# Query and key parts laid out head by head in DRAM, with two buffers in two attention stages and the query stores issued by ScalarE

## The reference, cut to what matters

```
q = (layernorm(x) @ Wq + bq), k = (ctx @ Wk + bk), v = (ctx @ Wv + bv)   # 8 x 512 x 256, 16 heads of 16
scores = einsum('bhqd,bhkd->bhqk', q, k) * scale                        # per head 512 x 512
out = softmax(scores) @ v                                               # then @ Wo + bo, added to x
```

## Time and profile before

| | us |
|---|---|
| median of 3 runs | 4700.8 (4699.31 to 4715.89) |
| the profiled execution | 4706.52 |
| its span | 4704.8 |
| a0: projections, then first work of the loop | 10.5 to 175.0 |
| a2: the same | 2925.2 to 3080.2 |
| a3: the same | 3831.2 to 3986.8 |

### The profile page before, as it was taken

One profiled execution on the slowest core, in us unless ns is written; L12 is line 12 of the kernel. 1 busy time (PEld: TensorE's weight loads), 2 busy tenths in 40 slices (PEclk: granted clock), 3 DMA queues, 4 the chain that ended last, 5 costly groups with the idle time before them and its releaser, 6 DMA issues. The chain is left out here.

```text
span 4704.8 us, 82799 instructions
## 1 busy us (share of the span) xinstructions
PE 3914.7 (83%) x30525; PEld 2826.9 (60%) x30525; DVE 3099.6 (66%) x7110; ACT 2060.3 (44%) x3636; POOL 796.3 (17%) x510
## 2 busy tenths in 40 slices
PE   6599999699367999785499996669988974999899
PEld 5244444588365777674388885535555663455577
DVE  7466664546656666545466664668867884988687
ACT  2155555134113333342154443247776851677511
POOL 4333330501341000000023323210000021000000
PEclk8699999599668999897599998869998997899999
DMA  6333331201320000010244545412210024121100
GB/s 205 102 98 101 101 96 41 88 21 44 106 77 32 18 18 18 28 43 31 72 126 123 130 125 144 166 60 66 67 37 14 1 71 148 55 66 65 34 19 19
DMA packets 202874, 337.94 MB, mean 72 GB/s; under 512 B 26036, under 2 KB 119781, under 8 KB 202566
## 3 DMA queue, kind: packets, MB, share of 16 engines
q1 hardware_dynamic: 186680, 306.61, 20.4%
q0 software_dynamic: 15888, 27.23, 2.8%
HBM read 242.42 MB, written 107.01 MB: 74 GB/s over the span
## 5 line engine op out<-in xcount | busy, mean ns | idle before, releaser
L1904 ACT ACTIVATE a_pT<-a_psS 128x512 f32<-128x512 f32 x1536 | 835.9, 598 | 405.0 <-PE a_psS L1790 399.6
L1976 DVE TENSOR_REDUCE a_mx<-a_psA 128x1 f32<-128x512 f32 x1024 | 656.6, 685 | 88.1 <-PE a_psA L1768 87.8
L1768 PE MATMUL a_psA<-a_ks,a_qs 48*128 48x512 f32 (+1 forms) x1536 | 404.4, 522 | 160.9 <-PEq L46 59.0
L1805 PE MATMUL a_psZ<-a_pT,a_V 128*17 128x128 f32 x12288 | 488.4, 278 | 0.0
L1972 DVE CUSTOM_DVE_ANT_0 a_scored<-a_psA,a_hide_q 128x512 bf16<-128x512 f32 x512 | 332.6, 688 | 193.4 <-PE a_psA L1768 192.3
L1805 PEld LDWEIGHTS a_psZ<-a_pT,a_V 128*17 128x17 f32 x12288 | 272.6, 97 | 270.8 <-issue 161.7
L1768 PEld LDWEIGHTS a_psA<-a_ks,a_qs 48*128 48x128 f32 (+1 forms) x1536 | 151.2, 192 | 408.7 <-issue 176.0
L1790 PE MATMUL a_psS<-a_qs,a_ks 50*128 50x512 f32 (+1 forms) x1536 | 319.1, 409 | 3.2 <-ACT a_pT L1904 0.8
L3244 DVE SCALAR_TENSOR_TENSOR ex_h<-ex_psU,ex_ub,ex_sg 128x512 f32<-128x512 f32 x129 | 96.9, 751 | 188.6 <-PE ex_psU L159 181.6
L1988 POOL TENSOR_TENSOR X<-X,a_osb 128x512 f32<-128x512 f32 x48 | 61.2, 1280 | 941.1 <-ACT a_osb L1891 923.1
L3190 ACT CAST ex_w_h<-X 128x1024 fp32r<-128x1024 f32 x102 | 106.1, 1041 | 149.3 <-DMA X<-in_L_ffn_gw 145.3
(11 more groups left out here) (606 smaller groups left out, 10257.4 us busy)
## 6 DMA issues: line engine op xcount, KB each, us to landing
a_k_parts<-a_p_kp SPq DMA_DIRECT2D x96, 256.0 KB
a_q_parts<-a_p_qp SPq DMA_DIRECT2D x96, 256.0 KB
a_qs<-a_q_parts SPq DMA_DIRECT2D x192, 128.0 KB
a_ks<-a_k_parts SPq DMA_DIRECT2D x192, 128.0 KB
X<-in_L_ffn_gw SPq DMA_DIRECT2D x36, 512.0 KB, 4.5
X<-in_L_ffn_up_w SPq DMA_DIRECT2D x36, 512.0 KB, 3.3
X<-in_L_ffn_down_w SPq DMA_DIRECT2D x36, 512.0 KB, 3.8
top_rows<-blank_rows SPq DMA_DIRECT2D x32, 514.0 KB, 11.3
```

The costliest lines, as they stand in the source:

```text
L1768: nc.tensor.matmul(psA[:, unit(a, par) % 3], qs[r, g % ring, p % 2, q * P:(q + 1) * P], ks[r, g % ring, p % 2], start=True, stop=True).the ...
L1805: last = nc.tensor.matmul(psZ[q * VP:q * VP + VW, g % 2, j * P:(j + 1) * P], V[:, b, kt, g % NG * GH + j, :], pT[:, p % 2, par, kt, q * P: ...
L1904: nc.scalar.activation(pT[:, p % 2, par, kt, :], psS[:, unit(t, par) % 3], ACT.Exp).then_inc(exp_done, 1)
L1976: nc.vector.tensor_reduce(mx[:, p // 2 % 2, par, p % 2, q:q + 1], psA[:, unit(a, par) % 3], AX_X, ALU.max).then_inc(a_used, 1)
```

## The change

In DRAM, `q_parts` and `k_parts` have the head ahead of the feature. A store then writes 128 consecutive rows. A load of a group has three DMAs for each stack and half in place of two: each takes one part of two heads, so none reads its source twice; 12 DMAs of 64 KB in place of 4 of 128 KB and 4 of 64 KB. In a2 and a3 `kp` and `qp` have two buffers, with a semaphore for each; a0 keeps one. The stores of the queries move from SyncE's program to ScalarE's, behind the copy of the next batch's tokens (`scalar_high`) and a wait for the low part of Q.

```diff
@@ resident_projections
-        kp, qp = sb("kp", [P, 2, KD, S], F32R), sb("qp", [P, 2, KD, S], F32R)
+        kp, qp = sb("kp", [P, buffers, 2, KD, S], F32R), sb("qp", [P, buffers, 2, KD, S], F32R)
...
+        def store(eng, parts, dram, stored):
+            for n in range(2):
+                for m in range(KD):
+                    heads = dram[n, m * P // DH:(m + 1) * P // DH].rearrange("h d t -> (h d) t")
+                    eng.dma_start(heads, parts[:, n, m].bitcast(F32)).then_inc(stored, 16)
...
-                            heads = dram[n, :, m * P // DH:(m + 1) * P // DH].rearrange("d h t -> h d t")
-                            sp.dma_start(heads, parts[:, n, m].bitcast(F32)).then_inc(stored, 16)
...
                     sp.wait_ge(k_low, b + 1)
-                    store(kp, k_dram[:, b], k_stored)
-                    sp.wait_ge(q_low, b + 1)
-                    store(qp, q_dram[:, b], q_stored)
+                    store(sp, kp[:, b % buffers], k_dram[:, b], k_stored[b % buffers])
                     if b == 4:
-                        sp.wait_ge(k_stored, 64 * b)
-                        sp.wait_ge(q_stored, 64 * b)
+                        for stored in k_stored + q_stored:
+                            sp.wait_ge(stored, 64 * b // buffers)
                     prepare.loads(sp, b)
...
                 def high_part(in_psum, ps, parts, bias, stored, done, b):
                     act.wait_ge(in_psum, b + 1)
-                    if b >= 1:
-                        act.wait_ge(stored, 64 * b)
+                    if b >= buffers:
+                        act.wait_ge(stored[b % buffers], 64 * (b // buffers))
...
                     high_part(q_in_psum, psQ, qp, bqs, q_stored, q_high, b)
                     if b + 1 < B:
                         f.scalar_high(act, b + 1, 0)
+                    act.wait_ge(q_low, b + 1)
+                    store(act, qp[:, b % buffers], q_dram[:, b], q_stored[b % buffers])
@@ attention_by_pairs
-        q_dram = nc.dram_tensor(nm + "q_parts", [2, B, DH, H, S], F32).ap()
-        k_dram = nc.dram_tensor(nm + "k_parts", [2, B, DH, H, S], F32).ap()
+        q_dram = nc.dram_tensor(nm + "q_parts", [2, B, H, DH, S], F32).ap()
+        k_dram = nc.dram_tensor(nm + "k_parts", [2, B, H, DH, S], F32).ap()
...
-                    return dram[part:part + 1, b, :, first:first + 2].rearrange("r d h t -> r d (h t)")
-                for stack, start, src in ((qs, 0, heads(q_dram, 0).to_broadcast([2, DH, 2 * S])), (qs, 2 * DH, heads(q_dram, 1)),
-                                          (ks, 0, heads(k_dram, 1)), (ks, DH, heads(k_dram, 0).to_broadcast([2, DH, 2 * S]))):
-                    rows = slice(64 * par + start, 64 * par + start + src.shape[0] * DH)
-                    sp.dma_start(stack[rows, slot].bitcast(F32).rearrange("p j t -> p (j t)"), src).then_inc(group_loaded[slot], 16)
+                    return dram[part, b, first:first + 2].rearrange("h d t -> d h t")
+                for stack, third, src in ((qs, 0, heads(q_dram, 0)), (qs, 1, heads(q_dram, 0)), (qs, 2, heads(q_dram, 1)),
+                                          (ks, 0, heads(k_dram, 1)), (ks, 1, heads(k_dram, 0)), (ks, 2, heads(k_dram, 0))):
+                    rows = slice(64 * par + third * DH, 64 * par + (third + 1) * DH)
+                    sp.dma_start(stack[rows, slot].bitcast(F32), src).then_inc(group_loaded[slot], 16)
...
+        (the call: buffers = 1 if hidden is not None else 2)
```

More of the change, by code:

```diff
@@ L1350, with resident_projections @@
 LEAD = 2 * STEPS
-def resident_projections(nc, A, G, nm, w, q_scale, q_dram, k_dram, V, wo, bo, prepare):
+def resident_projections(nc, A, G, nm, w, q_scale, q_dram, k_dram, V, wo, bo, buffers, prepare):
     with ExitStack() as ctx:
@@ L1369, in resident_projections @@
         cT_h, cT_l = sb("cT_h", [P, 2, KD, S], F32R), sb("cT_l", [P, 2, KD, S], F32R)
-        kp, qp = sb("kp", [P, 2, KD, S], F32R), sb("qp", [P, 2, KD, S], F32R)
+        kp, qp = sb("kp", [P, buffers, 2, KD, S], F32R), sb("qp", [P, buffers, 2, KD, S], F32R)
         w_loaded = {n: sem(n + "_loaded") for n in names}
         w_high, w_low, small_loaded, scaled = sem("w_high"), sem("w_low"), sem("small_loaded"), sem("scaled")
-        cT_loaded, k_stored, q_stored = [sem("cT_loaded0"), sem("cT_loaded1")], sem("k_stored"), sem("q_stored")
+        cT_loaded, k_stored, q_stored = [sem("cT_loaded0"), sem("cT_loaded1")], [sem(f"k_stored{n}") for n in range(buffers)], [sem(f"q_stored{n}") for n in range(buffers)]
         cT_high, cT_low, k_in_psum, v_in_psum, q_in_psum, v_taken, k_high, k_low, q_high, q_low = (
@@ L1394, in _ @@
                 prepare.sync(sp)
-                def store(parts, dram, stored):
-                    for n in range(2):
-                        for m in range(KD):
-                            heads = dram[n, :, m * P // DH:(m + 1) * P // DH].rearrange("d h t -> h d t")
-                            sp.dma_start(heads, parts[:, n, m].bitcast(F32)).then_inc(stored, 16)
                 for b in range(B):
@@ L1406, in _ @@
                     sp.wait_ge(k_low, b + 1)
-                    store(kp, k_dram[:, b], k_stored)
-                    sp.wait_ge(q_low, b + 1)
-                    store(qp, q_dram[:, b], q_stored)
+                    store(sp, kp[:, b % buffers], k_dram[:, b], k_stored[b % buffers])
                     if b == 4:
-                        sp.wait_ge(k_stored, 64 * b)
-                        sp.wait_ge(q_stored, 64 * b)
+                        for stored in k_stored + q_stored:
+                            sp.wait_ge(stored, 64 * b // buffers)
                     prepare.loads(sp, b)
-                sp.wait_ge(k_stored, 64 * B)
-                sp.wait_ge(q_stored, 64 * B)
+                for stored in k_stored + q_stored:
+                    sp.wait_ge(stored, 64 * B // buffers)
                 sp.wait_ge(small_loaded, 16 * len(smalls))
@@ L1466, in high_part @@
                     act.wait_ge(in_psum, b + 1)
-                    if b >= 1:
-                        act.wait_ge(stored, 64 * b)
+                    if b >= buffers:
+                        act.wait_ge(stored[b % buffers], 64 * (b // buffers))
                     for m in range(KD):
-                        nc.scalar.activation(parts[:, 0, m, :], ps[:, m, :], ACT.Identity, bias=bias[:, m:m + 1]).then_inc(done, 1)
+                        nc.scalar.activation(parts[:, b % buffers, 0, m, :], ps[:, m, :], ACT.Identity, bias=bias[:, m:m + 1]).then_inc(done, 1)
                 f.scalar_roots(act, 0)
@@ L1505, in low_part @@
                         dve.wait_ge(high_done, 2 * b + m + 1)
-                        last = nc.vector.scalar_tensor_tensor(parts[:, 1, m, :], ps[:, m, :], bias[:, m:m + 1],
-                                                              parts[:, 0, m, :].bitcast(F32), ALU.add, ALU.subtract)
+                        last = nc.vector.scalar_tensor_tensor(parts[:, b % buffers, 1, m, :], ps[:, m, :], bias[:, m:m + 1],
+                                                              parts[:, b % buffers, 0, m, :].bitcast(F32), ALU.add, ALU.subtract)
                     last.then_inc(done, 1)
@@ L1550, in attention_by_pairs @@
     ROWS = max_row + 2
-    LOADS = 2 * (4 + (added is not None))
+    LOADS = 2 * (6 + (added is not None))
     ring = 4 if hidden is not None else 5
     with ExitStack() as ctx:
-        q_dram = nc.dram_tensor(nm + "q_parts", [2, B, DH, H, S], F32).ap()
-        k_dram = nc.dram_tensor(nm + "k_parts", [2, B, DH, H, S], F32).ap()
+        q_dram = nc.dram_tensor(nm + "q_parts", [2, B, H, DH, S], F32).ap()
+        k_dram = nc.dram_tensor(nm + "k_parts", [2, B, H, DH, S], F32).ap()
         sb = lambda n, s, d=F32: ctx.enter_context(nc.sbuf_tensor(nm + n, s, d))
@@ L1680, in prepare_loads @@
                 load_group(sp, b - 4)
-        resident_projections(nc, A, G, nm + "p_", w, q_scale, q_dram, k_dram, V, wo, bo,
+        resident_projections(nc, A, G, nm + "p_", w, q_scale, q_dram, k_dram, V, wo, bo, 1 if hidden is not None else 2,
                              Prepare(prepare_sync, prepare_loads, prepare_pool, prepare_vector))
```

## The result

The changed kernel takes 4570.7 us in the median of four runs (4567.7 to 4572.8), beside 4702.5 for the kernel before in the same session: a ratio of 0.971, 95% interval 0.969 to 0.973. The forecast was 4570. The profiled execution took 4569.46 us with a span of 4567.5, against a span of 4704.8 before.

The account below looks back on a forecast made before the run. Projection halves wait for DMA, stores on 8 engines and doubled loads on two. Terms 46 + 45 + 33 + 7 + 6.6 = 137.6, less 7 for queueing, 130.6; 4700.8 - 130.6 = 4570 us, range 4540 to 4625.

Parts of the forecast that it names:

- a share of 0.57: Early a2 batches: DMA share 0.57 at 199 GB/s means 9.1 engines' worth, stores on 8 engines, a period of 13.1 us.
- The rate, 21.8 GB/s an engine: Early a2 batches: 199 GB/s over 9.1 engines' worth of work, used for the transfer times.
- the second period: a2 once loads come in: kp copies 20.9 us apart; doubled loads on two engines, 560 KB in 21 us at 27 GB/s.
- Halves of a2 and a3: Projection halves: batches of 11.1 us and a shorter stretch from last root to loop save 46 and 45 us.
- What would have shown it: Signs: a2 kp copies 11 us apart without DMA waits, share about 0.65 at over 230 GB/s, under 30 us root to loop.
- Predicted 33: a0's half: earlier mask makes the last qp some 20 us earlier, tail of 10.1 replaces 22.9: together 33 us saved.
- One buffer was called enough: a0's half: a key store would land some 5 us after issue, 2 us before the next copy is due.
- ScalarE's issues: Projections: four query issues at 565 to 630 ns take 2.3 to 2.5 us, fit into 3.34 us before the root, cost nothing.
- The bound named for the other side: Projections: at the crowded 5.98 us for four, ScalarE's query issues cost 2.6 us in each of 21 periods, 55 us.
- slower rival: Loops of a2 and a3: SyncE becomes the bound, 12 issues at over 0.94 us; 4725 us or more, chance 0.03.
- Loops: Attention loops: spread loads save 6.6 us in a0 and 7 in a3, whose four groups take 50.2 us; a2 nothing.
- the 7 us of queueing: Taken off the summed gain: 0.3 us in each of 21 periods.

Follow-up runs that it names:

- experiment 5: A kernel that only moves data, output x: outermost numbers 128, 16, 12, 8, 4, 2 gave DMA shares 1.03, 1.00, 0.76, 0.52, 0.26, 0.13.
- experiment 3: The changed kernel with an unused row behind each head in DRAM, so stores write 8 x 16 rows again: 4645.8 us, ratio 0.987.
- experiment 4: The changed kernel with eight of its twelve 64 KB loads a group reading their source twice again: 4636.6 us, ratio 0.985.
- Experiment 8: The changed kernel with single kp and qp buffers in a2 and a3 too: 4566.8 us, ratio 0.970.
- experiment 1: The kernel before with the new layout alone (head-by-head tensors, merged stores, twelve loads), single buffers, query stores on SyncE: 4568.6 us, ratio 0.971.
- experiment 7: The changed kernel with the query stores back on SyncE, both buffers kept: 4581.1 us, ratio 0.973.
- experiment 6: The changed kernel again, unaltered, measured beside other variants: 4563.4 us, ratio 0.971.
- experiments 7 to 9: experiment 7, Experiment 8, and the changed kernel with a0's second and third masks fetched one batch earlier, the last at 4558.0 us, ratio 0.968.

## Why the prediction was right

**Engines by shape.** The inference from a share of 0.57 (eight engines full, the rest nearly idle) is shown: experiment 5 measures the share for each outermost number, 3 brings the old regime back by the shape of the store alone, 4 does it for the loads at unchanged size. The rate, 21.8 GB/s an engine, lies within the 21.3 to 26.5 of experiment 5. There it is lower with 16 engines at work than with two, so the 27 GB/s that the second period needed is not far from what a doubled load shows. The sums took a KB of 1024 bytes for 1000, which makes their transfer times 2.4% too short; no term turns on it. By the Trainium skill, "DMA: Bandwidth & Descriptors", section "Why a DMA increments its semaphore by 16 and not by 1", the number of engines is the largest up to 16 that divides the slowest dimension of both sides; the store of 12 blocks agrees with that, with a share of 0.76.

**Halves of a2 and a3.** Predicted 46 and 45, measured 46.6 and 46.9. Period 10.9 us (11.1 predicted), last root to loop 2999.1 - 2974.8 = 24.3 us (24). Copies to `kp` have no DMA wait. What would have shown it did, with 0.73 at 258 GB/s for the share, more than the 0.65 named.

**a0.** Predicted 33, measured 38.9. The mask of the earlier trace rows was issued at 98.2 and used at 107.4 (placed at 101, landing after 9), the last copy to `qp` came at 128.0, 24.1 us earlier rather than 20, and the tail behind it took 8.1 us where 10.1 was counted. One buffer was called enough with an argument on key stores; for those it holds, but copies to `qp` wait 14.3 us for query stores, five times, the longest 4.88. Experiment 8 says that in a2 such waits cost nothing; in a0 two buffers were not tried.

**ScalarE's issues.** They cost nothing, as said, though on another ground than the price used: 565 to 630 ns was the price of an 8 x 16 store, the merged one issues in 326 at least. Four take 2.2 to 3.3 us in a2 and a3, just inside the 3.34. The bound named for the other side, 5.98 us for four, is what experiment 3 shows (5.3 to 6.2), with roots late.

**Twelve loads, slower rival.** The rival counted on dearer issues. Three loads issue in 1.3 to 1.4 us, a group with its maxima in 6.9 of 12.55 (SyncE's timeline in a2's loop):

```profile
3104.21 1.30 SPq L1745 DMA_DIRECT2D a_qs<-a_npartsT  x2
3105.62 1.27 SPq L1594 DMA_DIRECT2D a_qs<-a_q_parts  x3
3106.93 1.36 SPq L1594 DMA_DIRECT2D a_ks<-a_k_parts  x3
3108.33 1.35 SPq L1594 DMA_DIRECT2D a_qs<-a_q_parts  x3
3109.73 1.37 SPq L1594 DMA_DIRECT2D a_ks<-a_k_parts  x3
```

That is 0.45 us a load, against 0.53 for a load before the change. The Trainium skill (same page, "Rules for kernel authors") advises one large transfer over many small ones and calls those under 64 KB mostly overhead. Here the loads shrank from 128 to 64 KB and experiment 1 gained with them, while experiment 4 keeps the 64 KB and loses: at this size the shape decided. No run here has loads of the old size on 16 engines.

**Loops.** a0 gained 7.8 and a3 6.3 us against 6.6 and 7; the four groups in a3 take 50.23 us, as said (ACT's timeline after):

```profile
3971.74 0.24 ACT L1875 CAST a_npartsT<-a_psZ 32x128 fp32r<-32x128 f32 x1
4021.97 0.24 ACT L1875 CAST a_npartsT<-a_psZ 32x128 fp32r<-32x128 f32 x1
```

a2's 4.4 us were not foreseen. 4.1 of them lie in one group: ACT's maxima of the loop's third and fourth groups, before:

```profile
3125.66 0.25 ACT L1874 CAST a_npartsT<-a_psZ 32x128 fp32r<-32x128 f32 x1 [0.30 <-PE a_psZ L1819]
3141.15 0.24 ACT L1874 CAST a_npartsT<-a_psZ 32x128 fp32r<-32x128 f32 x1
```

and after:

```profile
3044.29 0.26 ACT L1875 CAST a_npartsT<-a_psZ 32x128 fp32r<-32x128 f32 x1
3055.68 0.24 ACT L1875 CAST a_npartsT<-a_psZ 32x128 fp32r<-32x128 f32 x1
```

15.5 us became 11.4. TensorE's granted clock, 0.50 (its lower level, 1.2 GHz) over the first 50 us of the loop before, rose a group sooner after (0.55 over the same 50), with PE busy 34.2 of the 50 us in both. In experiment 7 it is 0.50 over these 50 us again, and the loop took 430.6. What decides it I did not test.

**The sum.** The parts touched gained 150.9 us, and 148.3 in experiment 6, where 130.6 was forecast. The terms in the sum were too small: the 7 us of queueing did not appear, the a0 half was 6 us short, and a2's loop (4.4), counted at nothing, and the halves of a2 and a3 (2.5) make up nearly all the rest. In the first profile 13.6 us came back in unchanged code, 12.3 of them in the piece of experiment 6 with the lower clock, which no term foresaw. The terms that were too small and the clock worked against each other. That the median came out within 1 us of the forecast is thus partly luck; the difference of the medians was 131.8 us there and 140.1 in experiment 6. And the prediction gave the two buffers and ScalarE's queue no separate price: they are worth nothing that shows and some 5 us.

## What to carry to other kernels

Read the DMA share as a possible count of engines: a steady 0.57, 0.26 or 0.13 with engines waiting for transfers was here the sign that a shape, not the memory, was the limit. It is a sign and no proof, since the 0.50 of the last two sections in experiment 5 came from issues (139 GB/s, where stores on 8 engines moved 199), and the compute-bound loops before the change had 0.21 and 0.20. Then look at the outermost number of each DMA's access on both sides. Lay the DRAM tensor out so that it merges to 128 rows, and write a doubled load as two. Buffers and another issuing engine come after that, and each should be timed without the other.

## What was not expected of the hardware

Issue time goes with the shape and not only with the engines: 344 ns at least for `128x512` and 585 for `16x8x512`, both on 16 engines. The stages between, which were never touched, took 2115.1 to 2130.6 us in ten profiles, as much as experiments 7 to 9 wanted to tell apart; some 12 us of it are one piece at a granted clock of 0.86 in place of 0.93. The lengths of the parts told the kernels apart where the totals could not.
